# Layer norms with epsilon added on GpSimd, affine steps fused into VectorE operations, one power for a norm of a norm, and new orders of work

## The reference, cut to what matters

```
def _ln(x, g, b):                       # inside the cross attention block
    m = mean(x); v = var(x)
    return (x - m) * rsqrt(v + 1e-05) * g + b

x = x + cross(_layernorm(x), ctx)       # a plain norm, and then inside cross:
def cross(xx, ee):
    x = _ln(xx, ln1_g, ln1_b)           # a norm of a norm
    x = x + mha(x, x, ...)              # norms of its own: of x (twice), of x_out
    x = _ln(x, ln2_g, ln2_b)
    return x + mha(x, ee, ...)          # norms of x, of ee, of x_out
```

## Time and profile before

| | |
|---|---|
| median of 3 runs | 2383.33 us (2377.45 to 2383.9) |
| profiled execution, first to last instruction | 2313.3 us |
| own time of the profiled execution | the profile gives only its span; the median less the span is 70.0 us |
| instructions | 66487 |
| mean granted TensorE clock | 0.931 |
| TensorE / VectorE / ScalarE / GpSimd busy | 85% / 69% / 54% / 49% |

### The profile page before, as it was taken

The page is one execution under the profiler, slowest core; times in us unless marked ns, Lnnn a source line. Parts: engine busy times, 40 slices in busy tenths (PEclk is TensorE's granted clock), DMA queues, the critical chain, the costliest instruction groups (busy, mean ns, idle before and its releaser), DMA issues.

```text
span 2313.3 us, 66487 instructions
## 1 busy us (share of the span) xinstructions
PE 1964.8 (85%) x27020; PEld 1633.0 (71%) x27020; DVE 1603.6 (69%) x4253; ACT 1255.5 (54%) x2880; POOL 1124.5 (49%) x1336
## 2 busy tenths in 40 slices
PE   5899978889788998899999689667588999898982
PEld 3767757677576776777777478667477888697882
DVE  6589786787857888678767835665889666854232
ACT  5457875467654777657765435234344455443551
POOL 2775336742367633675255354351877222234466
PEclk8999989999899999999999789789699999998996
DMA  4000000000000000000010065797011000026994
GB/s 142 5 6 2 2 1 6 6 2 2 1 3 6 3 2 1 5 5 3 2 38 13 8 187 167 222 235 266 25 28 31 4 9 9 4 83 228 349 315 125
DMA packets 98047, 147.35 MB, mean 64 GB/s; under 512 B 32016, under 2 KB 72464, under 8 KB 97488
## 3 DMA queue, kind: packets, MB, share of 16 engines
q1 hardware_dynamic: 88656, 124.48, 17.0%
q0 software_dynamic: 9088, 18.63, 3.3%
HBM read 126.49 MB, written 16.58 MB: 62 GB/s over the span
## 4 chain that ended last, share of the span: by engine, by line
PE 53%; DVE 24%; issue 8%; POOL 8%; ACT 4%; DMA 2%; SPq 0%; POOLq 0%; DVEq 0%; ACTq 0%
PE PS L2108 5%; PE PS L2092 5%; PE PS L1578 3%; PE PS L1584 3%; PE PS L1060 3%; PE PS L674 3%; PE PS L660 2%; POOL GOT L1736 2%; DVE mx L1054 2%; DVE P L1056 2%; PE PS L1067 2%; PE PS L1075 2%; PE PS L1036 2%; DVE zo L636 2%; PE PS L1171 2%
## 5 line engine op out<-in xcount | busy, mean ns | idle before, releaser
L2122 ACT ACTIVATE wh<-PS,we 128x128 f32<-128x128 f32 x624 | 176.0, 373 | 231.5 <-PE PS L2092 231.0
L1990 POOL DMA_INDIRECT wx<-x,INV x156 | 153.1, 981 | 204.5 <-PE PS L2099 106.0
L2092 PE MATMUL PS<-wxT,we 128*128 128x128 f32 x1248 | 176.3, 289 | 42.5 <-issue 35.1
L1054 DVE TENSOR_REDUCE mx<-PS 128x8 f32<-128x512 f32 x256 | 176.1, 688 | 45.8 <-PE PS L1049 24.0
L640 POOL TENSOR_TENSOR xrs<-xrs,Cs 128x2 f32<-128x2 f32 x112 | 82.0, 732 | 255.0 <-DVE xrs L632 252.7
L2108 PE MATMUL PS<-we,wh 128*128 128x128 f32 x1248 | 181.4, 290 | 22.8 <-DVE wxT L2140 21.1
L2092 PEld LDWEIGHTS PS<-wxT,we 128*128 128x128 f32 x1248 | 161.0, 202 | 49.5 <-issue 48.7
L2108 PEld LDWEIGHTS PS<-we,wh 128*128 128x128 f32 x1248 | 163.8, 202 | 32.2 <-DVE wxT L2140 29.3
L1056 DVE TENSOR_TENSOR P<-PS,mx 128x512 f32<-128x512 f32 x256 | 177.1, 692 | 8.9
L1060 PE MATMUL PS<-Cs,P 128*128 128x128 f32 x1024 | 157.5, 287 | 28.1 <-ACT P L1473 21.0
L1500 POOL TENSOR_TENSOR km<-qk,Cs 128x1024 f32<-128x1024 f32 x64 | 121.1, 1898 | 119.8 <-ACT qk L1458 48.1
(11 more groups left out here) (359 smaller groups left out, 5427.2 us busy)
## 6 DMA issues: line engine op xcount, KB each, us to landing
we<-in_wf SPq DMA_DIRECT2D x78, 578.0 KB, 5.6
we<-in_wl SPq DMA_DIRECT2D x78, 578.0 KB, 5.9
yf<-wy SPq DMA_DIRECT2D x78, 64.0 KB, 5.1
ys<-wy SPq DMA_DIRECT2D x78, 64.0 KB, 5.1
x<-X SPq DMA_DIRECT2D x32, 128.0 KB, 1.9
R<-in_wa SPq DMA_DIRECT2D x1, 3072.0 KB, 14.6
wx<-x,INV POOLq DMA_INDIRECT x156, 5.5
X<-in_x SPq DMA_DIRECT2D x4, 512.0 KB, 15.0
```

The source lines that it names most:

```text
L1054: e.tensor_reduce(A.mx[r], S3, AX, ALU.max).then_inc(*o.inc())
L1990: e.indirect_dma_start(out=WB[s].x[q // NS % NX], out_offset=None, in_=x1[k], in_offset=bass.IndirectOffsetOnAxis(ap=INV[k % NH][:, q - T0 ...
L2092: i = e.matmul(ps(s, 1)[:, 128 * f:128 * f + 128], w[:, 128 * f:128 * f + 128], B.xT, True, True)
L2122: i = e.activation(B.h[:, 128 * f:128 * f + 128], ps(s, 1)[:, 128 * f:128 * f + 128], ACT.Relu, bias=w[:, 512 + f:513 + f])
```

## The change

`dve_stats` no longer adds epsilon; `pool_pow` does so on GpSimd, ahead of the power. The norm of a norm takes variance times (1 + epsilon) plus epsilon squared, and one power of that. The gain and bias of ln1 and ln2 move from GpSimd to VectorE: `dve_affine` computes (x - mean) * gain per tile, before the reciprocal deviation is known, and `dve_shift` computes that times `rs` plus bias, in place of `dve_norm`. The statistics of the context (y) move on VectorE from behind var.x to behind the first attention's last head step, and their power on GpSimd from behind rstd.x to behind m_xr.0. The small buffer r2 goes. All strings of `ORDER`, in both phases, are new.

```
         "dve":
-            "... d_x var.x m_yvar z.x var.a0 z.a0 ... m_xo.0 var.b0 z.b0 var.mid m_y z.mid var.a1 ..."
+            "... d_x var.x m_x1 var.a0 z.a0 ... a_on.0.1.1 m_yvar m_xo.0 var.b0 z.b0 var.mid m_y m_x3 var.a1 ..."
         "pool":
-            "... vz.x rstd.x m_yrstd m_x1 rstd.a0 ... m_xr.0 rstd.mid m_x3 rstd.a1 ..."
+            "... vz.x rstd.x rstd.a0 ... m_xr.0 m_yrstd rstd.mid rstd.a1 ..."
@@ dve_stats
-            i.then_inc(*o.inc())
-            e.wait_ge(*o.now())
-            return e.tensor_scalar(sm.rs, sm.mv[:, :, 1], EPS, None, ALU.add)
+            return i
+        def dve_affine(e, dst, src, sm, g):
+            o = own["dve"]
+            for t in range(NT):
+                i = e.scalar_tensor_tensor(out=dst[:, t, :], in0=src[:, t, :], scalar=sm.mv[:, t, 0:1], in1=rw(g), op0=ALU.subtract, op1=ALU.mult)
+            i.then_inc(*o.inc())
+            return o.now()
+        def dve_shift(e, dst, sm, b):
+            for t in range(NT):
+                i = e.scalar_tensor_tensor(out=dst[:, t, :], in0=dst[:, t, :], scalar=sm.rs[:, t:t + 1], in1=rw(b), op0=ALU.mult, op1=ALU.add)
+            return i
-        def pool_pow(e, sm):
+        def pool_pow(e, sm, twice=False):
+            o = own["pool"]
+            if twice:
+                e.tensor_scalar(sm.rs, sm.mv[:, :, 1], 1 + EPS, EPS * EPS, ALU.mult, ALU.add).then_inc(*o.inc())
+            else:
+                e.tensor_scalar(sm.rs, sm.mv[:, :, 1], EPS, None, ALU.add).then_inc(*o.inc())
+            e.wait_ge(*o.now())
             return e.tensor_tensor(sm.rs, sm.rs, HALF.broadcast_to([128, NT]), ALU.pow)
@@ dve_cross
             dve_stats(e, xi(G), B.sm).then_inc(*sig.inc(G, "var", "x"))
-            (wait for the context; its statistics)
+            e.wait_ge(*sig.at(G, "var", "x"))
+            scaled = dve_affine(e, B.x1, xi(G), B.sm, "ln1g")
             yield
             e.wait_ge(*sig.at(G, "rstd", "x"))
-            dve_norm(e, B.x1, xi(G), B.sm).then_inc(*sig.inc(G, "z", "x"))
+            e.wait_ge(*scaled)
+            dve_shift(e, B.x1, B.sm, "ln1b").then_inc(*sig.inc(G, "m_x1"))
             (the same for mid: ln2g and ln2b into B.x3)
@@ pool_cross
-            (six operations for rstd.x; two for the gain and bias of x1; two for those of x3)
+            pool_pow(e, B.sm, True).then_inc(*sig.inc(G, "rstd", "x"))
```

More of the change, by code:

```diff
@@ L84 @@
         "dve":
[4 rows of a table removed]
[4 rows of a table added]
         "pool":
-            "rstd.d d_edge d_sq d_kb d_ak.0 d_ak.1 d_mm d_ak.2 d_ak.3 d_ak.4 d_osq d_orn vz.x rstd.x m_yrstd m_x1 rstd.a0 m_xb.0 a_mk.0.0 a_mk.0.1 "
-            "a_mk.1.0 a_mk.1.1 rstd.b0 m_xr.0 rstd.mid m_x3 rstd.a1 m_xb.1 rstd.b1 m_xr.1 m_xi rstd.t",
+            "rstd.d d_edge d_sq d_kb d_ak.0 d_ak.1 d_mm d_ak.2 d_ak.3 d_ak.4 d_osq d_orn vz.x rstd.x rstd.a0 m_xb.0 a_mk.0.0 a_mk.0.1 a_mk.1.0 a_mk.1.1 rstd.b0 "
+            "m_xr.0 m_yrstd rstd.mid rstd.a1 m_xb.1 rstd.b1 m_xr.1 m_xi rstd.t",
     },
@@ L176 @@
[L176 to L179, removed]
@@ new lines @@
+        "pool":
+            "012300332211002233023110022000100332220032200333311221332211110331100011222230333002122111302333111100223300112230030112220033302221113331110000222233"
+            "003322001122113311330002211332003110002200122200332200333221133221113301133000112222113000333210221112333311110022331010223300011222330030221121333111"
+            "000022220033330011221133220033110112233231100100022003320022333002233112233111223311011000112322233300012221110333231111002233001122330001122200333022"
+            "211133311100002222333300112200112233110033112202333001102200100222330022300332233112233111011330001121122230333002122111032331311001223300112233000112"
+            "2233003022211133311100002222333301111231",
@@ L1271, in dve_mha @@
                     yield
+            if a == 0:
+                e.wait_ge(*l_e.landed(G))
+                dve_stats(e, B.eT, B.sm2).then_inc(*sig.inc(G, "m_yvar"))
+                yield
             e.wait_ge(*sig.at(G, "m_li1", a))
@@ L1328, in dve_cross @@
             dve_stats(e, B.xb, B.sm).then_inc(*sig.inc(G, "var", "mid"))
+            e.wait_ge(*sig.at(G, "var", "mid"))
+            scaled = dve_affine(e, B.x3, B.xb, B.sm, "ln2g")
             yield
@@ L1335, in dve_cross @@
             e.wait_ge(*sig.at(G, "rstd", "mid"))
-            dve_norm(e, B.x3, B.xb, B.sm).then_inc(*sig.inc(G, "z", "mid"))
+            e.wait_ge(*scaled)
+            dve_shift(e, B.x3, B.sm, "ln2b").then_inc(*sig.inc(G, "m_x3"))
             yield
@@ L1351, in pool_cross @@
             e.wait_ge(*sig.at(G, "var", "x"))
-            pool_pow(e, B.sm).then_inc(*o.inc())
-            e.wait_ge(*o.now())
-            e.tensor_tensor(B.r2, B.sm.rs, B.sm.rs, ALU.mult).then_inc(*o.inc())
-            e.wait_ge(*o.now())
-            e.tensor_tensor(B.r2, B.r2, B.sm.mv[:, :, 1], ALU.mult).then_inc(*o.inc())
-            e.wait_ge(*o.now())
-            e.tensor_scalar(B.r2, B.r2, EPS, None, ALU.add).then_inc(*o.inc())
-            e.wait_ge(*o.now())
-            e.tensor_tensor(B.r2, B.r2, HALF.broadcast_to([128, NT]), ALU.pow).then_inc(*o.inc())
-            e.wait_ge(*o.now())
-            e.tensor_tensor(B.sm.rs, B.sm.rs, B.r2, ALU.mult).then_inc(*sig.inc(G, "rstd", "x"))
+            pool_pow(e, B.sm, True).then_inc(*sig.inc(G, "rstd", "x"))
+            yield
+            yield from pool_mha(e, s, G, 0, B.x1)
             yield
@@ L1366, in pool_cross @@
             yield
-            e.wait_ge(*sig.at(G, "z", "x"))
-            e.tensor_tensor(B.x1, B.x1, bc(rw("ln1g"), 1, NT), ALU.mult).then_inc(*o.inc())
-            e.wait_ge(*o.now())
-            e.tensor_tensor(B.x1, B.x1, bc(rw("ln1b"), 1, NT), ALU.add).then_inc(*sig.inc(G, "m_x1"))
-            yield
-            yield from pool_mha(e, s, G, 0, B.x1)
-            yield
             e.wait_ge(*sig.at(G, "var", "mid"))
             pool_pow(e, B.sm).then_inc(*sig.inc(G, "rstd", "mid"))
-            yield
-            e.wait_ge(*sig.at(G, "z", "mid"))
-            e.tensor_tensor(B.x3, B.x3, bc(rw("ln2g"), 1, NT), ALU.mult).then_inc(*o.inc())
-            e.wait_ge(*o.now())
-            e.tensor_tensor(B.x3, B.x3, bc(rw("ln2b"), 1, NT), ALU.add).then_inc(*sig.inc(G, "m_x3"))
             yield
```

133 lines of the change are left out of this document (64 added, 69 removed), and 8 rows, old and new, of the table STEPS.

## The result

The changed kernel takes 2451.5 us (median of 4 runs, 2448.6 to 2456.2), the kernel before beside it 2382.0 us: ratio 1.0285, with a 95% interval of 1.0255 to 1.0315. It is 69.5 us slower, where I had forecast 22 us faster; the time lies outside my range (2336 to 2399). A second set of runs gave 2446.8 against 2377.4 us, 1.0293 [1.0263, 1.0323].

A forecast was written before the change was run, and what follows sets the result against it. TensorE was taken to bound phase one, VectorE close behind. Off the chain came 34.9 us in phase one and 9.8 in phase last, together 44.7; half, 22 us, from 2383.3 gave 2361 us, range 2336 to 2399.

The forecast's parts named there:

- What goes, and what of it is on the chain: Removed epsilon additions and GpSimd norm, gain and bias work: 48.8 us off phase one's chain, 16.5 us off phase last's.
- What comes: GpSimd additions and VectorE affine calls add 6.1 and 7.8 us to phase one's chain, at most 6.7 to phase last's.
- rival (b): Affine call and GpSimd's power fail to overlap because one engine stands still: 2370 us, chance 0.14.
- the rule that I weighed: VectorE with two SBUF inputs and GpSimd reading SBUF share ports; the loser stands still for the whole operation.
- How much of it reaches the end: Of 44.7 us off the chain in both phases, half was taken to reach the end: 22 us, giving 2361 us.
- rival (c): Nothing arrives, as TensorE's written-out order replaces each norm's wait: 2381 us, chance 0.11.
- Rival (d): Slower by the new order, all four slots in the delta rule together: 36 us lost, 2397 us, chance 0.17.
- three stretches: Delta-rule stretches of phase one with TensorE busy 81, 78 and 87 of 100 us, each to lose 12 us more.
- The test that I had set: Forecast wrong if phase one is not shorter, or over 10 us of the difference come from phase last.
- The sum's base: Span of 2313.3 us plus 70.0 us around it, untouched by the change: 2383.3 us.
- the latency sign: From GpSimd's start on rstd.x to a0's statistics: some 1.8 us where the chain took 4.8 us.

The follow-up runs named there:

- edits_old_orders: All edits of arithmetic and engine, with both orders as in the kernel before and the context's statistics at their old place; ratio to the kernel before 1.0017.
- after_last_old: The changed kernel with only the order of the last phase put back to the old one; ratio to the kernel before 1.0255.
- tuned_one: All edits, the old last-phase order, and phase one's old order with single turns of the four engines moved a few places; ratio to the kernel before 1.0050.

## Why the prediction was wrong

*What goes, and what of it is on the chain*: right in the count of what goes, wrong in what would follow from it. L632 is gone, and VectorE's busy time is down by 74 us in the changed kernel and by 36 in edits_old_orders (I had said 20 to 65). But TensorE's waits for norms, which I had taken as the time to be won, stay at 31.2 of 32.3 us with all edits in the old orders; that they fell to 4.6 us in the changed kernel is the new order's doing.

*What comes*: the sizes held. The addition on GpSimd and the affine and shift calls, by source, in after_last_old (count, ns min/median/max):

```profile
L655 POOL TENSOR_SCALAR xrs<-xmv x96: 210/218/588, 143.6 to 1234.4; 128x2 f32<-128x2 f32 x96
...
L640 DVE SCALAR_TENSOR_TENSOR x<-X,xmv,Rw x32: 342/349/678, 129.9 to 1072.6; 128x128 f32<-128x128 f32 x32
...
L646 DVE SCALAR_TENSOR_TENSOR x<-x,xrs,Rw x64: 318/345/1132, 136.4 to 1163.7; 128x128 f32<-128x128 f32 x64
```

218, 349 and 345 ns where I had taken 220, 347 and 347. So rival (b) falls: the affine call doesn't stand still beside GpSimd, though single ones take up to 1132 ns: 7 of these 128 instructions take over 400 ns, and a GpSimd operation runs during some 80% or more of each of the seven. On the rule that I weighed from the Trainium skill (SBUF — State Buffer, "SBUF: two separate sides"): medians at the unhindered duration and rare long maxima fit a lock that is met seldom.

*How much of it reaches the end* is the step that failed first. I took half of what left the chain, 22 us; in the old orders nothing arrived (1.0017, phase one 4 us shorter, the last one 6 longer). In edits_old_orders TensorE's waits for the norms were the old ones, 19.0 + 22.0 us up to 1180 us against 22.2 + 19.5. My reading is that each engine takes its turns in a written sequence, so an earlier statistic only waits longer for its turn. It is argued and not shown: tuned_one, made to test it, gained nothing. As a result it is rival (c) for the edits, which I gave 0.11.

*Rival (d)*. The second and larger failure is that the sum of the forecast has no term for the new orders: it put them at nothing, and left them to rival (d). That rival named the right mechanism with 0.17 and priced it too low: the slots closer together, all in the delta rule at once, nothing of another slot to fill in. I asked for 12 us in each of three stretches, 36 us. Measured are 59 us (with the same arithmetic), and mostly not in the three stretches I had pointed at (there TensorE lost 4.5, 1.4 and 5.9 us of 100, and at 76.6, 76.4 and 81.3 us none fell under the 75 that I had set as the sign) but behind them, from 650 to 800 and from 950 to 1100 us above all. I had read "fed badly" off the busy share without asking what limits the feed. The rows "issue" behind L674 were in the trace of before and I passed them over, as some 9 of 111 us idle. With them the first narrow stretch of 50 us, at the supply's pace, would have hinted that a second one beside it can't be had for nothing.

*The order of the last phase* I left out altogether. I wrote that over 10 us from the last phase would prove the forecast wrong and the order its cause; it was 39 to 45 us with the old arithmetic, 12 to 24 with the edits behind the old order of phase one, and 19 to 20 in the changed kernel itself. The test that I had set was right, and the case belonged among the rivals.

*The sum's base*: I took 70 us around the span. There are 2 (the profiled run of the changed kernel took 2456.2 us, its span is 2454.4). The trace of before has a span of 2313.3 us as on the chips where this kernel takes 2307 to 2316 us, while the timed runs took 2383, so it is most likely from another chip than they are. That moved the base and not the difference, though the share of the last phase was understated by 66 to 69 us. A small slip beside it: the four terms of the latency sign (0.22 + 0.07 + 0.7 + 0.69) make 1.7 us, not 1.8.

## What to carry to other kernels

When a diff brings a new hand-written or planned order, price the order by itself before the arithmetic: here the arithmetic was worth nothing and the two orders cost 2.9%. Look in the old order for the stretch where every slot would run the same part, and ask which resource saturates there. For TensorE that includes its instructions: matmul records of under about 30 ns each need wide ones between them, and fewer, wider matmuls help where none are at hand.

## What was not expected of the hardware

TensorE's instruction stream gave 128 multiplication records with their weight loads per 3.77 us (13 rounds), and the pauses show as "issue". While big loads were arriving, two pauses of 2.1 and 2.8 us came even at 32 ns a record.

Chips differ by 3% on this kernel (2307 to 2316 and 2377 to 2382 us), nearly all of it in the last phase (1195 to 1201 against 1132 to 1135 us with its old order).

Two edits that cost 0.7% each alone cost 0.2% together.
